# Attention by whole batches in a fused cross-attention and mixture-of-experts kernel

## What is computed

```
x = x + attention(layernorm(x), ctx)      # q = ln(x) Wq + bq; k, v from ctx; scores masked by two masks
x = x + ffn(layernorm(x))
ffn(y) = geglu(y Ws1 + bs1) Ws2 + bs2     # shared expert, hidden width 512
       + sum over the 2 chosen of 12 experts of w_e * (geglu(y We1[e] + be1[e]) We2[e] + be2[e])   # hidden 768
w = softmax of the two largest of (y Wr + br) / 1.5
```

## Time and profile before

| | us |
|---|---|
| median of three runs | 694.4 (692.1 to 694.56) |
| the profiled execution | 694.07 |
| its span, first to last instruction | 692.2 |
| mean granted TensorE clock | 0.957 of 2.4 GHz |
| busy: TensorE / VectorE / ScalarE / GpSimd | 640.6 / 468.6 / 305.4 / 349.8 |
| start of the masks of pairs 0, 1, 5, 6, 7 | 19.4, 45.8, 153.3, 179.8, 213.9 |
| last normalisation of attention | 254.6 |
| first expert's bias | 298.7 |

### The profile page before, as it was taken

How to read it: one execution, slowest core, us unless ns; L and a number is a source line. 1 busy time by engine, 2 the same in 40 slices (tenths; PEclk the granted TensorE clock), 3 DMA queues, 4 the chain that set the end, 5 groups by cost and what they waited for, 6 DMA issues and landing times.

```text
span 692.2 us, 14875 instructions
## 1 busy us (share of the span) xinstructions
PE 640.6 (93%) x4418; PEld 537.2 (78%) x4419; DVE 468.6 (68%) x1037; ACT 305.4 (44%) x677; POOL 349.8 (51%) x403
## 2 busy tenths in 40 slices
PE   8899999999978879679999999999999999999695
PEld 7787887887856669567888788878887888889595
DVE  7688677688754946666667667766766766774467
ACT  5465556556543343423444444444443444443232
POOL 3881011011054763877789389479886683003553
PEclk9899999999997888889999999999999999999799
DMA  8827524516921043342654344444465231101433
GB/s 280 305 104 263 213 87 156 212 39 251 349 77 62 16 152 107 129 145 77 213 178 172 122 160 171 139 157 148 165 212 174 83 121 38 38 16 50 119 97 117
DMA packets 47910, 98.95 MB, mean 143 GB/s; under 512 B 4736, under 2 KB 23808, under 8 KB 47872
## 3 DMA queue, kind: packets, MB, share of 16 engines
q1 hardware_dynamic: 36192, 50.40, 20.6%
q0 software_dynamic: 10976, 47.72, 20.4%
q10 hardware_dynamic: 704, 0.33, 0.2%
HBM read 57.15 MB, written 39.19 MB: 139 GB/s over the span
## 4 chain that ended last, share of the span: by engine, by line
PE 71%; DVE 13%; issue 5%; ACT 4%; another core or an unknown queue 3%; POOL 1%; DVEq 1%; DMA 1%; ACTq 0%; SPq 0%; POOLq 0%
PE ps_s L788 25%; PE ps_o L821 9%; PE ps_o L822 4%; PE ps_t L584 4%; PE ps_o L596 3%; PE ps_s L572 3%; PE ps_s L750 3%; PE ps_t L798 3%; PE ps_t L511 2%; DVE nmax L1311 2%; PE ps_s L567 1%; PE ps_x L511 1%; PE ps_s L798 1%; PE ps_x L809 1%
## 5 line engine op out<-in xcount | busy, mean ns | idle before, releaser
L788 PE MATMUL ps_s<-ring,xTh 128*128 x516 | 153.0, 418 | 0.0
L1787 POOL TENSOR_TENSOR ring<-stage,ring 128x512 fp32r<-128x512 f32 x80 | 100.6, 1291 | 1.2
L788 PEld LDWEIGHTS ps_s<-ring,xTh 128*128 128x128 f32 x516 | 89.2, 191 | 14.8 <-issue 0.3
L821 PE MATMUL ps_o<-ring,hTh 128*128 x258 | 96.7, 412 | 3.5 <-DVE hTl L1615 3.5
L1606 DVE TENSOR_TENSOR ag<-ps_s,up_bias 128x512 f32<-128x512 f32 x129 | 89.0, 690 | 13.1 <-PE ps_s L788 10.4
L1775 POOL TENSOR_TENSOR ve<-mv,eps 128x2 f32<-128x2 f32 x16 | 4.0, 250 | 161.8 <-DVE mv L1343 148.3
L788 PE MATMUL ps_s<-ring,xTl 128*128 x258 | 80.5, 393 | 0.0
L982 ACT ACTIVATE probT<-ps_t 128x512 f32<-128x512 f32 x64 | 38.3, 598 | 80.4 <-PE ps_t L584 74.0
L822 PE MATMUL ps_o<-ring,hTl 128*128 x258 | 72.6, 281 | 0.0
L1969 POOL DMA_INDIRECT gath<-rows_out,idx_out x32 | 31.9, 998 | 76.3 <-DMA rows_out<-y_row 56.6
L1094 ACT ACTIVATE ps_s<-ag 128x256 f32<-128x256 f32 x129 | 50.2, 389 | 40.6 <-DVE ag L1606 39.2
(11 more groups left out here) (274 smaller groups left out, 1464.1 us busy)
## 6 DMA issues: line engine op xcount, KB each, us to landing
rows_in<-y_row SPq DMA_DIRECT2D x8, 3328.0 KB, 12.2
stage<-in_w POOLq DMA_DIRECT2D x12, 1536.0 KB
stage<-in_w POOLq DMA_DIRECT2D x12, 768.0 KB, 5.3
up_bias<-in_bias POOLq DMA_DIRECT2D x12, 768.0 KB, 4.5
xrow<-rows_in SPq DMA_DIRECT2D x43, 128.0 KB, 2.2
rows_out<-y_row SPq DMA_DIRECT2D x43, 128.0 KB, 1.7
cbuf<-in_ctx SPq DMA_DIRECT2D x8, 256.0 KB, 3.1
xn_all<-xn2p SPq DMA_DIRECT2D x8, 256.0 KB
```

The costliest lines, as they stand in the source:

```text
L788: last = pe_.matmul(ps_s[:, i, :], x[:, c, :], weights(place, off + c * 2 * HR + i * 2 * D, 2 * D), start=n == 0, stop=n == 5)
L821: pe_.matmul(ps_o[:, :], hTh[i][:, c, :], weights(place, a, 2 * D), start=i == 0 and c == 0, stop=False)
L1787: last = pool.tensor_tensor(lo_ap[:, c:c + PIECE], src[:, c:c + PIECE], hi_ap[:, c:c + PIECE].bitcast(f32), ALU.subtract)
```

## The change

Scores and values are made for a whole batch at once: four groups of rows, four of output columns. The transposes of a batch stand behind the scores of the next, so the lag is one batch. probT holds a whole batch and moves to free room of the weight ring. The steps are spread anew over each pair, with new orders on ScalarE and VectorE; in the last pair TensorE gets a filler of four products after each transposes; on GpSimd the scatters are paced by `pt_ready` instead of `scores_ready`, and those of tiles 8 to 11 come after the down weights of expert 0. The diff, cut:

```diff
-    probT = put("probT", [P, 2, 4, P], f32, low)
+    fr = [ring_at + ((RING - 1) * SLOT_W + 2 * (W1S + W2S)) * 4]
+    probT = put("probT", [P, 4, 4, P], f32, fr)
...
         if last:
-            return ["r", "n", "l"]
+            return ["n", "r", "l"]
         if first:
             return AHEAD + PROJ + AHEAD
-        todo = ["k0"] + (["n"] if batch_in(p) is not None else []) + ["k1", "q0", "q1", "r", "v", "l"]
-        return todo + ([] if isinstance(p, int) and p == PAIRS - 2 else AHEAD)
+        todo = ["k0", "k1", "q0"] + (["n"] if batch_in(p) is not None else []) + ["q1", "v"]
+        return todo + (["r", "l"] if isinstance(p, int) and p == PAIRS - 2 else ["cT", "r", "xT", "l"])
...
-            def scores(p, par, n):
+            def scores(p, par, b):
...
-                    pe.wait_ge(shifted, U - 1)
-                for jj in range(2):
+                    pe.wait_ge(shifted, (p * 2 + b) * 2)
+                for j in range(4):
...
-                        for j in (2 * u, 2 * u + 1):
+                        for j in range(4):
...
+            def values(b, par, batch):
+                pe.wait_ge(pt_copied, batch * 4 + 4)
...
                 for g in range(4):
-                    for jj in range(2):
+                    for j in range(4):
...
-            SPIN = 1
+            SPIN = 4
...
+                def filler():
+                    if last:
+                        pe.wait_ge(xb_free, base_of(p, first))
+                        spin(SPIN, ps_x[:, 0:D])
...
+                scores(p, par, 0)
...
+                    prev = p * 2 - 1
+                    prob_transposes(prev, 0)
+                    put("k0", (0,))
+                    filler()
+                    prob_transposes(prev, 1)
+                    put("k0", (1,))
+                    filler()
+                    prob_transposes(prev, 2)
+                    put("k1", (0,))
+                    filler()
+                    prob_transposes(prev, 3)
+                    put("k1", (1,))
+                    filler()
+                    values(1, 1 - par, prev)
+                    put("q0", (0,))
+                    filler()
+                    out_transposes(prev)
+                    put("q0", (1,))
+                    if not last:
+                        put("n")
+                scores(p, par, 1)
...
+                values(0, par, prev)
+                if tail:
+                    put("cT", again=first)
+                if last:
+                    put("n")
+                put("r")
+                out_transposes(prev)
+                if tail:
+                    put("xT", again=first)
+                put("l")
```

Between `scores(p, par, 1)` and `values(0, par, prev)` stand `prob_transposes(prev, 0..3)` with halves of `q1` and `v` and a filler behind each. Router `l` now waits only for `r`'s copy. ScalarE and VectorE in a pair that is neither the first nor the last:

```diff
+                    prob_copy(prev, 0)
+                    prob_copy(prev, 1)
                     put("k0")
+                    prob_copy(prev, 2)
+                    prob_copy(prev, 3)
+                    put("k1")
+                    out_copy(prev)
                     exp(p * 4, 0)
+                    exp(p * 4 + 1, 1)
+                    put("q0")
+                prev = p * 2
+                prob_copy(prev, 0)
+                prob_copy(prev, 1)
                 put("q1")
+                prob_copy(prev, 2)
+                prob_copy(prev, 3)
+                put("v")
+                out_copy(prev)
                 exp(p * 4 + 2, 2)
+                put("cT", first)
+                put("r")
                 exp(p * 4 + 3, 3)
                 put("xT", first)
...
+                softmax_shift(p * 4, 0, p * 2, (lambda: put("cT")) if first else None)
+                softmax_shift(p * 4 + 1, 1, p * 2, lambda: put("k0"))
+                put("k1")
+                if not first:
+                    if further:
+                        ln1_stats(p + 2)
+                    norm(p - 1, 1)
+                    residual(p - 1, 1)
+                put("q0")
                 if not last:
                     put("n")
                 if isinstance(p, int) and p == PAIRS - 3:
                     choose(0, 0)
+                if last:
+                    choose(0, 1)
+                    choose(1, 1)
+                softmax_shift(p * 4 + 2, 2, p * 2 + 1)
+                if not first:
+                    ln2_apply(p - 1)
                 if isinstance(p, int) and p == PAIRS - 2:
                     row_numbers(0)
+                softmax_shift(p * 4 + 3, 3, p * 2 + 1, lambda: put("q1"))
+                if further:
+                    put("cT", first)
+                    ln1_apply(p + 2)
                 if last:
                     put("n")
                 norm(p, 0)
+                if further:
+                    put("xT", first)
+                residual(p, 0)
+                put("l")
```

The seam on TensorE, and GpSimd:

```diff
+            prob_transposes(B - 1, 0)
             pe.wait_ge(xb_free, PAIR_STEPS_END - 1)
             x_group(0)
+            prob_transposes(B - 1, 1)
             pe.wait_ge(converted, 1)
             pe.wait_ge(shifted, UNITS)
+            spin(SPIN, ps_s[:, 3, 0:D])
+            prob_transposes(B - 1, 2)
             chunk_ups(0, 0, SH)
+            prob_transposes(B - 1, 3)
+            chunk_ups(0, 1, SH)
+            values(1, 1, B - 1)
+            chunk_ups(0, 2, SH)
             out_transposes(B - 1)
             chunk_ups(0, 3, SH)
...
+            def paced_scatters(tiles, step):
+                for i, t in enumerate(tiles):
+                    gp.wait_ge(pt_ready, step + i + 1)
+                    scatter(t)
...
                 if last:
-                    gp.wait_ge(scores_ready, 4 * p + 1)
-                    for t in (6, 7):
-                        scatter(t)
+                    paced_scatters(range(3, 7), (p * 2 - 1) * 4)
...
-                    for n in range(1, 4):
-                        gp.wait_ge(scores_ready, 4 * p + n + 1)
-                        for t in (2 * n - 2, 2 * n - 1):
-                            scatter(t)
+                    paced_scatters(range(3), p * 8 + 1)
                 if last:
+                    paced_scatters((7,), p * 8)
                     gp.wait_ge(xb_free, base_of(p, first))
                     first_w1()
...
             gp.wait_ge(converted, 2)
             load_raw2(1)
+            gp.wait_ge(xn2_saved, 16 * 6)
+            gp.wait_ge(rows_ready, 2)
+            for t in range(8, 12):
+                scatter(t)
```

More of the change, by code:

```diff
@@ L525, in step, with router @@
                     last.then_inc(xb_ready, 1)
-            def router(s, q, idx, bank):
+            def router(s, q, idx, bank, router_free=None):
                 if s == "r":
@@ L576, in scores, with prob_transposes @@
                 last.then_inc(scores_ready, 1)
[L578 to L582, removed]
+            def prob_transposes(batch, j):
+                pe.wait_ge(exp_done, batch * 2 + j // 2 + 1)
+                if not (isinstance(batch, int) and batch == 0 and j == 0):
+                    pe.wait_ge(pt_copied, batch * 4 + j)
                 for g in range(4):
-                    last = pe_.transpose(ps_t[:, 0, g * P:(g + 1) * P], prob[n % 2][:, jj, g, :], ident)
+                    last = pe_.transpose(ps_t[:, 0, g * P:(g + 1) * P], prob[j // 2][:, j % 2, g, :], ident)
                 last.then_inc(pt_ready, 1)
[L587 to L590, removed]
+            def values(b, par, batch):
+                pe.wait_ge(pt_copied, batch * 4 + 4)
+                if not (isinstance(batch, int) and batch == 0):
                     pe.wait_ge(normed, batch)
                 for g in range(4):
-                    for jj in range(2):
[L594 to L597, removed]
+                    for j in range(4):
+                        last = pe_.matmul(ps_o[32 * j:32 * j + VW, g * P:(g + 1) * P], v_sb[par][:, b, 4 * g + j, :],
+                                          probT[:, j, g, :], start=True, stop=True)
                         if g == 3:
@@ L976, in step, with prob_copy @@
                         .then_inc(xb_free, 1)
[L978 to L982 removed]
+            def prob_copy(batch, j):
+                sc.wait_ge(pt_ready, batch * 4 + j + 1)
+                if not (isinstance(batch, int) and batch == 0):
+                    sc.wait_ge(pv_done, batch * 4)
+                act.activation(probT[:, j, :, :], ps_t[:, 0, :].rearrange("p (g t) -> p g t", g=4),
                                ACT.Identity).then_inc(pt_copied, 1)
@@ L1452, in pair @@
                     row_numbers(0)
-                if last:
-                    choose(0, 1)
-                softmax_shift(p * 4 + 1, 1)
-                put("k1")
-                if not first:
-                    residual(p - 1, 1)
-                    if further:
-                        ln1_stats(p + 2)
-                    ln2_apply(p - 1)
-                if last:
-                    choose(1, 1)
-                softmax_shift(p * 4 + 2, 2)
-                put("q0")
+                softmax_shift(p * 4 + 3, 3, p * 2 + 1, lambda: put("q1"))
+                if further:
+                    put("cT", first)
```

(10 more changed lines are left out.)

167 lines of the change are left out of this document (46 added, 121 removed).

## The result

The changed kernel takes 708.6 us (median of four, 705.7 to 710.2) beside 694.5 of the kernel before (692.1 to 698.3): ratio 1.019, 95% interval 1.014 to 1.025. It is slower. The prediction was 686.0, with a range of 673 to 698.

A forecast was written before the change was run, and what follows sets the result against it. It took TensorE's matmul time and the transposes' loop through ScalarE's copy to bound attention. Terms -8.6 + 0 - 3 + 3 - 3 + 3.5 = -8.1 against 694.07 gave 686 us, range 673 to 698.

The forecast's parts named there:

- Four groups side by side: TensorE's scores: four row groups run at once, a batch in 8 rounds of 0.11 us, 0.9 us, full gain.
- Case B: Rival: slower, the four groups don't run side by side, pairs of 28.5 us, 707 us in all; chance 0.10.
- The halves at full clock: Pairs 1 to 4: first half of a pair 10.6 us, second half 14.1 us with TensorE waiting ahead of xT.
- Part by part, at full clock: Step pricing each part of a pair at full clock: 24.7 instead of 26.86 us, -8.6 us over four pairs.
- rival C: Gain given back at the seam: scatters stall once more, fillers run at half clock; +8, 694 us; chance 0.15.
- Pair 7, 40.0: Last pair with tail: norm starts at 40.0 us, before 40.7 with a stall of 3.4; work grows by 3 us.
- The stalls: ScalarE's waits beside scatters: 8.4 us scaled by 16/24, -3 us; behind it 3.75 becomes up to 7.5, +3.5 us.
- The seam, +3.5: Between attention and experts: 16 scatters in one run instead of 8, the stall there grows, +3.5 us.
- The cover of the moved scatters: GpSimd: scatters of tiles 8 to 11 fit an idle of 11.04 us, under 1 us to spare before tiles 12 to 15.
- Right: Signs: score rows of four 0.11 apart, masks to transposes 2.0, values 1.1, pairs 24.7, idle 1 to 2.5 us ahead of xT.
- Wrong: Signs: rows of two or 0.22 apart (B); pairs of 22.3; pair 7 and seam together over 84.85 us (C).
- A: The forecast itself, whole kernel: 677 to 690 us; chance 0.60.

The follow-up runs named there:

- e1: Changed kernel with 8 filler products on TensorE in the idle time ahead of the transposes to xT: ratio 0.9995, 692.8 us.
- e3: Changed kernel with VectorE's ln1_apply moved ahead and ScalarE's cT high part ahead of the exp of unit 2: ratio 0.978, 677.2 us.
- e2: Changed kernel with VectorE's ln1_apply moved ahead of cT's low part, behind the subtraction of unit 2: ratio 0.989, 687.5 us.
- e4: Changed kernel with one filler product at each place instead of four: ratio 1.012, 700.3 us.
- e16: Changed kernel with GpSimd waiting for all scatters' landing before tiles 2, 4, 6, 8 and 10: ratio 1.011, 703.2 us.
- e10: e3 with choose, ranks and positions of batch 1 reordered in pairs 6 and 7, two filler products, five around pair 6's out transposes: 0.979, 676.9 us.
- e15: e13 with GpSimd's conversion of the first expert's weights put off until attention's last subtraction: ratio 0.960, 667.5 us.
- e7: e3 with two filler products at each place of the last pair and tail instead of four: ratio 0.976.
- e11: e10 with fillers instead of shared-expert chunks between the tail's transposes, and VectorE's norm, ln2_apply and choose ahead: ratio 0.976, 674.1 us.
- e17: e14 with GpSimd's queue laid out anew around the pauses: ratio 0.984, 660.3 us, beside 671.5 for the kernel before.
- e5: e3 with the scatters of tiles 0 to 11 left out, their rows not written for the experts: ratio 0.969, 671.3 us.
- e12: e11 with the scatters of tiles 8 to 11 put ahead of GpSimd's last rstd: ratio 0.975, 673.1 us.
- e14: e13 with GpSimd waiting for all landings before every tile up to 11, so at most two scatters unbroken: ratio 0.968, 671.9 us.
- e18: The kernel of e17 unchanged, in a set of its own: ratio 0.966, 669.5 us, beside 693.7 for the kernel before.
- e13: e11 with GpSimd waiting for all scatters' landing before tiles 2, 4, 6, 8 and 10: ratio 0.971, 673.8 us.

## Why the prediction was wrong, step by step

**Four groups side by side: right.** 8 steps of 0.11, masks to transposes 2.0, values 1.1. By the prices of the earlier trace rows it took the right side. The Trainium skill's 62 ns a matmul ("TensorE: Matmul & The Clock Gate", section "Wait — 56ns, not 53.3ns?"), which the page gives for hardware decode off, would make, as an estimate, 2.0 us for the 32 score matmuls of a batch; they take 0.9, so that price doesn't hold for this kernel. No run here shows how the matmuls were decoded. Case B was refuted, though its 707 is the time that came.

**The halves at full clock: right.** First half 10.6, and 10.67 in e1 and 10.60 in e3. Second half 14.1, and 13.68; the idle time of 1 to 2.5 us ahead of xT, and 2.23, released by ln1_apply as it said.

**"Part by part, at full clock": the step that failed.** The prediction itself put an idle time of up to 2.5 us into every pair, where TensorE is idle for some 0.4 us a pair in the earlier trace rows (1.5 in 107), and then priced the next half at full clock, as if nothing followed from it. The half behind it took 13.6 us instead of 10.6. That is 3.0 us a pair in pairs 2 to 6 and 3.6 in pair 1, and some 3 in pair 7: 21 us, where the prediction was off by 22.6. With it pairs 1 to 4 would have been forecast at -8.6 + 12.6 = +4.0; they were +2.2, as each second half came out some 0.4 shorter than predicted. The earlier trace rows showed the lower clock in the last pairs, and the prediction priced it in pair 6 of the kernel before (1.5 us) and named it in rival C, but not behind the idle times that it had made itself. None of its rivals has the clock of pairs 1 to 5. The cause is shown for these pairs (e1, e2, e3); the fall is not certain each time, as one half in e4 and one in e16 kept the clock behind the same wait.

**Pair 7, 40.0: mis-sized by 9.5.** The filler steps were right (2.17 us, 2.15 predicted). Missed were the half clock at its start (masks to transposes 3.9 us instead of 2.0), the choice of experts ahead of shift 2, which stands beside GpSimd's conversion and takes 6.7 us there (3.5 in e10, ahead of it), ScalarE's copy of r, which waits 2.36 us for pos behind the last shift, and a wait of 4.26 us beside the scatters, which the prediction had booked under the stalls. They are not independent: e16 shows that the stall is what pushed the choice into the conversion. And the clock's 3 us of this pair are in the 21 above too. e15, with all but the stall mended, takes 39.8; that this is the predicted 40.0 is partly luck, as it still has a wait of 4.84 us, and two filler products where there were four.

**The stalls.** Two terms of -3 and +3.5 stood for them. In the changed kernel they are 4.26 us in pair 7 and 2.21 and 2.88 in the seam, 9.4 in all against 12.2 of the earlier trace rows, and behind attention 5.1 against 3.75: within the bounds. Scaling by 16/24 had no ground: e3, e7 and e10 have the same scatters and waits of 4.04, 5.41 and 7.01 us, by when the awaited work is done.

**The seam, +3.5: near.** +4.4, of which the stalls are 1.3 (5.09 us for 3.75); e11 takes 3 us off pair 7 and seam together by the order of the tail. How much the clock of 0.79 (0.81 before) costs was not tested. The cover of the moved scatters was thicker than the "under 1 us" of the prediction: GpSimd still waits 4.68 us for the numbers of tiles 12 to 15.

```profile
287.35 0.99 POOL L1889 DMA_INDIRECT rows_in<-xn_all,idx_top  x1 [4.68 <-DVE idx_top L1415]
```

**The last 2.6 us**, behind the first expert's bias, where nothing was changed, stay open. That stretch takes 393.5 us in the kernel before, 396.1 in the changed one and 392.4 to 397.1 in the others, but for e17 (384.1), so 2.6 us is within what the runs differ by.

**The signs that the prediction gave.** "Right" held in all its rows, but for the 24.7 of a pair. "Wrong" said that pair 7 and the seam together would be longer than 84.85 us: they are 98.1. But the forecast's own terms for the two (+3, +3.5 and a part of the stalls) make them some 5 us longer, so that sign could not tell C from A. Neither named the clock of the pairs.

## What to carry to other kernels

A change that replaces matmul time by waiting, on a kernel that keeps TensorE full, has to be priced with the clock: one wait of 2.2 us in each 27 cost 3 us more behind it, and the order of two steps on the helping engines, or zeros multiplied in the gap, gave it back. When a kernel gets slower, look first at the granted clock of each stage beside the idle times ahead of it. What is saved ahead of a wait that ends at its own time is lost in it: look at when a wait ends, not how long it is.

## What the runs showed of the hardware

- **The clock.** With 2.23 us idle ahead of xT the granted clock was 0.50 for about half of the next 13.6 us (mean 0.75) in pairs 2 to 6 of the changed kernel; one such half in e4 and one in e16 stayed at 1.00. With 1.50 (e2) and 0.56 (e3) it stayed at 1.00 in nearly all pairs.
- **Indirect DMAs on GpSimd.** Beside runs of them ScalarE and VectorE stand for 2 to 8 us although nothing that the profile shows holds them, and TensorE's matmuls come with gaps of 0.4 to 0.7 us (e3, from 252.8 to 255.6). Beside eight in a row most of these waits end 11.4 to 11.8 us after the first of the eight, in e3, e5, e10 and the changed kernel. Others don't: 9.2 us after it in the kernel before (251.38 in the earlier trace rows), 3.5 and 7.2 in e12, and 8.5 after the first of six in e10 (VectorE, 3.36 us). With the row broken after every second one, for 2.2 us, e14 has none over 0.6 us up to tile 11, and e18 one of 2.87; after every fourth they stayed in e13 and e15, while e16 lost that of pair 7. Gathers at the end of the kernel do the same (5.75 and 3.55 us). One set of six showed none of it, and there the kernel before took 671.5 us instead of 691 to 695. What it is, is not settled; that the chip of that set differs in this alone was not tested.
- **VectorE beside GpSimd.** Small operations on SBUF took up to 3.09 us instead of 0.20, and ln2_apply 3.69 us instead of 0.73 in e10, while GpSimd converted weights. A maximum that reads PSUM kept its 1.21 us.
- **The fastest version** against its own runs is e15_late, 0.960 of the kernel before (0.955 to 0.964; e18 is 0.966), and nearly 6% less than the changed kernel. It still has waits beside the scatters and beside the gathers, up to 5.7 us each.
